# The first unit's maxima move from the front of the second attention into the first mixture

## The reference

```python
qkv = x @ Wqkv + bqkv
q, k, v = jnp.split(qkv, [D, D + KV], axis=-1)          # D = 256, KV = 64
q = q.reshape(b, s, H, HD)                              # H = 16 heads of HD = 16
k = jnp.tile(k.reshape(b, s, G, HD), (1, 1, H // G, 1)) # G = 4 shared keys
v = jnp.tile(v.reshape(b, s, G, HD), (1, 1, H // G, 1))
scores = jnp.einsum('bqhd,bkhd->bhqk', q, k) / HD
prob = jax.nn.softmax(scores, axis=-1)
out = jnp.einsum('bhqk,bkhd->bqhd', prob, v).reshape(b, s, D)
return out @ Wout + bout
```

## Time and profile before

| what | value |
| --- | --- |
| median of three runs | 2161.28 us (2160.81 to 2163.94) |
| profiled execution, its own time | 2152.04 us |
| span in the profile | 2150.0 us |
| mean granted clock, as a share of full speed | 0.986 |
| PE busy | 2080.3 us (97%) |
| DVE busy | 1460.8 us (68%) |
| ACT busy | 1221.3 us (57%) |
| POOL busy | 577.9 us (27%) |

### The profile page before, as it was taken

One profiled execution on the slowest core, in us unless ns is written; L12 is line 12 of the kernel. 1 busy time (PEld: TensorE's weight loads), 2 busy tenths in 40 slices (PEclk: granted clock), 3 DMA queues, 4 the chain that ended last, 5 costly groups with the idle time before them and its releaser, 6 DMA issues. The chain is left out here.

```text
span 2150.0 us, 33338 instructions
## 1 busy us (share of the span) xinstructions
PE 2080.3 (97%) x12160; PEld 1592.7 (74%) x12160; DVE 1460.8 (68%) x2761; ACT 1221.3 (57%) x2435; POOL 577.9 (27%) x679
## 2 busy tenths in 40 slices
PE   7999999999999999989999988999999899999997
PEld 6888888888788888877788873333334688778886
DVE  5666666677677666666656558999994556655555
ACT  5666666666556666554444443888887434444433
POOL 3444444444334444332222210000000112222221
PEclk9999999999999999999999996999999999999999
DMA  2000000000000000011111121101000111111111
GB/s 74 20 21 13 21 21 20 21 21 20 9 20 21 20 21 20 4 38 45 39 48 40 45 46 30 24 18 23 21 12 2 43 37 45 45 45 44 45 52 56
DMA packets 54309, 64.92 MB, mean 30 GB/s; under 512 B 9179, under 2 KB 34566, under 8 KB 54150
## 3 DMA queue, kind: packets, MB, share of 16 engines
q1 hardware_dynamic: 54150, 62.81, 10.4%
HBM read 52.68 MB, written 2.10 MB: 25 GB/s over the span
## 5 line engine op out<-in xcount | busy, mean ns | idle before, releaser
L862 POOL TENSOR_TENSOR a_pr<-a_pr,a_rinv 128x512 f32<-128x512 f32 (+3 forms) x384 | 312.8, 829 | 477.1 <-DVE a_rinv L1109 477.1
L86 PE MATMUL psum<-xh,g_hi_gu 128*128 128x512 f32 x928 | 377.8, 407 | 15.1 <-DVE xl L1092 8.9
L88 PE MATMUL psum<-xh,g_lo_gu 128*128 128x512 f32 x928 | 363.7, 392 | 0.0
L87 PE MATMUL psum<-xl,g_hi_gu 128*128 128x512 f32 x928 | 363.2, 391 | 0.0
L1830 DVE TENSOR_REDUCE a_negm<-psum 128x1 f32<-128x1024 f32 x256 | 309.7, 1223 | 17.5 <-PE psum L1697 16.5
L1190 POOL TENSOR_TENSOR g_lo_gu<-g_raw_gu,g_hi_gu 128x512 fp32r<-128x512 f32 x84 | 108.9, 1297 | 778.1 <-ACT g_hi_gu L1186 778.1
L1811 ACT ACTIVATE a_pt<-psum 128x512 f32<-128x512 f32 x512 | 276.4, 597 | 60.4 <-PE psum L1712 32.6
L1484 DVE TENSOR_TENSOR f_hl<-f_hid,f_hh 128x512 fp32r<-128x512 f32 x168 | 116.8, 695 | 238.4 <-ACT f_hh L1422 236.5
L1411 ACT ACTIVATE f_act_s<-psum,g_gu_bias 128x512 f32<-128x512 f32 x168 | 115.0, 685 | 277.7 <-PE psum L88 277.4
L1014 ACT ACTIVATE a_pr<-psum,a_negm 128x128 f32<-128x128 f32 (+7 forms) x256 | 190.2, 743 | 106.9 <-DVE a_negm L1099 102.9
L1021 ACT ACTIVATE a_pth<-psum 128x512 fp32r<-128x512 f32 (+3 forms) x384 | 174.9, 490 | 113.0 <-PE psum L921 110.3
(11 more groups left out here) (298 smaller groups left out, 4313.7 us busy)
## 6 DMA issues: line engine op xcount, KB each, us to landing
g_raw_gu<-in_gu SPq DMA_DIRECT2D x84, 256.0 KB, 2.8
f_raw_dn<-in_down SPq DMA_DIRECT2D x84, 128.0 KB, 2.0
g_raw_gu<-in_qkv SPq DMA_DIRECT2D x32, 256.0 KB, 2.8
a_wvr<-in_qkv SPq DMA_DIRECT2D x32, 128.0 KB, 2.4
a_wor<-in_o SPq DMA_DIRECT2D x32, 128.0 KB, 2.0
x_queries_qq<-x_qhi SPq DMA_DIRECT2D x128, 32.0 KB, 2.0
yT<-in_xT SPq DMA_DIRECT2D x4, 512.0 KB, 7.1
x_queries_qq<-x_qlo SPq DMA_DIRECT2D x64, 32.0 KB, 1.9
```

The source lines that it names most:

```text
L86: pe.matmul(out, a_hi, b_hi, start=first, stop=False)
L87: pe.matmul(out, a_hi, b_lo, start=False, stop=False)
L88: return pe.matmul(out, a_lo, b_hi, start=False, stop=last)
L862: pool.tensor_tensor(x, x, rinv[:, j:j + 1].to_broadcast([P, count * P]), ALU.mult).then_inc(p_done, 1)
```

## The change

Unit 0's 16 maxima leave `FIRST` and become side tasks of the first mixture, in tiles 37 to 44, two tasks for each half tile (one for each product, so both side banks). DVE reduces both banks in one instruction and raises `emptied` by two. For this the tasks before them are set closer: `root` at (31, 0) where it was at (31, 1), the `nb` tasks at (32, 0) to (33, 1), the `pj` and `vt` tasks from (34, 0) to (36, 1), and two `pj` tasks as second tasks at (33, 0) and (36, 0). SP copies the keys after `load(37)` and fetches unit 0's queries after `load(38)`; `p1` fetches units 1 and 2. In the second attention `turn(-1)` comes first, `FIRST` holds the eight maxima of unit 1, and PE adds two products to each of them whose result nothing reads. The copy of the second half's keys moves behind unit 0's maxima in SP's order. The query slots become four tensors, and `negm` is allocated outside the attention.

```diff
+class FirstMaxima:
+    COUNT = CH // P * G1
...
+    def tensor(self, pe, t, ring):
+        half, (q, g) = t[0], head_of(t[1])
+        p0, rows = g // 2 * HALFP, 3 * HD1
+        if t == (0, 0):
+            pe.wait_ge(self.side.k_in, self.side.K_LOADS)
+            pe.wait_ge(self.queries.q_in[0], 192)
+        o = free_bank(pe, ring, (self.name, t))
+        pe.matmul(o, self.queries.qq[0][p0:p0 + rows, g % 2, q * P:(q + 1) * P],
+                  self.side.ks[p0:p0 + rows, g % 2, half * CH:(half + 1) * CH], start=True, stop=True).then_inc(ring.filled, 1)
+    def scalar(self, act, t, ring):
+        pass
+    def vector(self, dve, t, ring):
+        if t[0] == 0:
+            return
+        q, g = head_of(t[1])
+        n = g * (CH // P) + q
+        dve.wait_ge(ring.filled, ring.count((self.name, t)))
+        dve.tensor_reduce(self.negm[:, 0, n:n + 1], self.both, AX.XY, ALU.max, negate=True).then_inc(ring.emptied, 2)
...
             for K in range(2, 2 * NT):
                 load(K)
+                for o in begins:
+                    if isinstance(o, QKVHalf) and K == NT + 9:
+                        o.sync(sp, ring)
+                    if isinstance(o, FirstMaxima) and K == NT + 10:
+                        o.queries.first(sp, o.side, ring)
             for o in begins:
                 if isinstance(o, QKVHalf):
-                    o.sync(sp, ring)
                     sp.wait_ge(o.k_in, o.K_LOADS)
...
-        FIRST = [(0, i) for i in range(STEPS)] + [(1, i) for i in range(STEPS // 2)]
+        FIRST = [(1, i) for i in range(STEPS // 2)]
...
-            sides[1].sync(sp)
-            queries.fetch(sp, Queries.AHEAD)
             for u in range(LAST + 1):
                 send_maxima(u)
                 if u == 0:
                     queries.fetch(sp, QSLOT - 1)
+                    sides[1].sync(sp)
...
+            turn(-1, False, True, room(ring.a_turn(-1, False, True)))
             for u, i in FIRST:
                 bank = room(ring.a_max())
                 for half in range(2):
                     maxima(u, i, half, bank)
-                if (u, i) == (0, STEPS - 1):
-                    turn(-1, False, True, room(ring.a_turn(-1, False, True)))
+                for n in range(2):
+                    pe.matmul(st_ps[:, n, :], ks[0][:, 0, 0:P], ks[0][:, 1, 0:CH], start=True, stop=True)
...
-                            **place(NT0 + 1, norm_slots(n1a) + PAUSE + tasks(x0, PROJECT))}
+                            **place(NT0 + 1, tasks(n1a, FORE + [("root",)]) + PAUSE + tasks(n1a, BACK) + tasks(x0, PROJECT[:6]))}
+                    for n, t in ((8, ("pj", 1, 0)), (14, ("pj", 1, 1))):
+                        plan[NT0 + 1 + n // 2, n % 2].append((x0, t))
+                    for n in range(m0.COUNT):
+                        plan[NT0 + 9 + n // 2, n % 2] = [(m0, (0, n)), (m0, (1, n))]
```

More of the change, by code:

```diff
@@ L1191, in remainder, with __init__, widen, fetch @@
                            ALU.subtract).then_inc(self.lo_done, 1)
+class Queries:
+    SLOTS, AHEAD = 4, 2
+    UNITS = [(b, j, c) for b in range(B) for j in range(H1 // G1) for c in range(S // CH)]
+    def __init__(self, ph, name, qhi, qlo):
+        self.ph, self.name, self.qhi, self.qlo = ph, name, qhi, qlo
+        self.qq = [ph.sb(f"{name}_qq0", [P, 2, CH], F32R)]
+        self.q_in = [ph.sem(f"{name}_q_in{s}") for s in range(self.SLOTS)]
+    def widen(self):
+        self.qq += [self.ph.sb(f"{self.name}_qq{s}", [P, 2, CH], F32R) for s in range(1, self.SLOTS)]
+    def fetch(self, sp, u):
+        b, j, c = self.UNITS[u]
+        t0, s = c * CH, u % self.SLOTS
+        for r in range(2):
+            for x, src in enumerate((self.qhi[b], self.qhi[b], self.qlo[b])):
+                for g in range(2):
+                    d0 = (j % 2 * G1 + r * 2 + g) * HD1
+                    p0 = r * HALFP + x * HD1
+                    sp.dma_start(self.qq[s][p0:p0 + HD1, g, :].bitcast(F32),
+                                 src[d0:d0 + HD1, j // 2, t0:t0 + CH].bitcast(F32)).then_inc(self.q_in[s], 16)
+    def sync(self, sp):
+        for u in range(1, 1 + self.AHEAD):
+            self.fetch(sp, u)
+    def first(self, sp, side, ring):
+        sp.wait_ge(ring.emptied, ring.count((side.name, ("pj", 0, 0))))
+        self.fetch(sp, 0)
@@ new lines, with head_of, __init__, has_bank @@
+GROUPS = (0, 2, 1, 3)
+def head_of(i):
+    return i // G1, GROUPS[i % G1]
+class FirstMaxima:
+    COUNT = CH // P * G1
+    def __init__(self, ph, name, queries):
+        self.name, self.queries = name, queries
+        self.negm = ph.sb(f"{name}_negm", [P, 2, self.COUNT])
+    @staticmethod
+    def has_bank(t):
+        return True
+    @staticmethod
+    def rounds(t):
+        return False
+    def tensor(self, pe, t, ring):
[16 more added lines that the diff above has]
+        dve.tensor_reduce(self.negm[:, 0, n:n + 1], self.both, AX.XY, ALU.max, negate=True).then_inc(ring.emptied, 2)
@@ L1269, in mixture @@
         after.ready = lambda s, ring: ((y_kept, (s // 2 + 1) * DT),)
+        for o in begins:
+            if isinstance(o, FirstMaxima):
+                o.both = side_ps[:, :, :]
         @block.sync
@@ L1510, in _, with grouped_attention @@
                             o.vector(dve)
[L1513 to L1541, removed]
+def grouped_attention(nc, tag, counters, queries, negm, sides, ks, vs, z, ident, psum, rear):
     ROWS = 3 * HD1
@@ L1614, in place @@
             def place(self):
-                if self.maxima < len(UNITS) * STEPS:
+                if self.maxima < MAXIMA:
                     self.n += 1
@@ L2007, in program @@
                 x.level(0)
[L2008 removed]
+                queries.widen()
                 with Phase(nc, "s1") as s:
```

33 lines of the change are left out of this document (16 added, 17 removed).

## The result

The changed kernel takes 2200.91 us (median of four, 2197.98 to 2205.19), the kernel before 2161.28 (2160.81 to 2163.94) on the same chip: ratio 1.0182, 95% interval 1.0164 to 1.0201. It is slower, as forecast, by 39.6 us where 10.7 were forecast, and outside the range (2160 to 2181). The profiled executions are 49.2 us apart in span (2150.0 and 2199.2).

A forecast was written before the change was run, and what follows sets the result against it. The prediction took PE to bound the mixture and DVE the maxima ahead of the second attention's loop. It summed 33.9 us paid in the mixture less 23.2 given back, +10.7, to 2172.0 us; range 2160 to 2181.

The forecast's parts named there:

- the waits: PE's new waits in the mixture: for side banks 16.8 us, for unit 0's queries 3.9, from closer tasks 5.8.
- 14.6 of 16.8: Tiles 38 to 44, (K, 0): PE waits 2.4 us each for side banks to be reduced, 16.8 us.
- 3.9 of 3.9: At (37, 0): the first maximum waits 3.9 us for unit 0's queries to land; bounds 1.5 and 5.9.
- 5.5 of 5.8: Tasks set closer: `root` +2.1 us, `pj` at (33, 0) 1.8, `pj` at (36, 0) 1.9; together 5.8.
- the products: Mixture: 32 added products of 512 columns at 0.23 us each, 7.4 us of PE.
- upper end of 12.5: Mixture: the added products at 0.39 us each, a whole length, if they don't overlap: 12.5 us.
- so my sum has no fall in it: Mixture: 2.4 us waits, shorter and between 9 us of unbroken products, add no slow-clock time to the sum.
- Rival 1: Clock falls at the waits: ten waits, each losing 1.7 us of products, make +17, 2189 us; chance 0.07.
- rival 2: Added products don't hold the clock, PE bounds ahead of the loop, only 16.8 us returned: +17.1, 2178; chance 0.07.
- I take 23.2, because PE has work there without a break: Second attention: the loop's tenth reduction ends 23.2 us earlier, with the added products free at full clock.
- The low end, 16.8: Second attention at 1.2 GHz: eight times 0.6 us lost and 1.5 us of loop start not saved; 16.8 returned.
- The 9.2 us: Median of the runs shown, 2161.28, is 9.2 us above the profiled execution; the same sum was put on it.

The follow-up runs named there:

- e2: Changed kernel, but DVE reduces the maximum of (K-1, 1) ahead of `keep_lo(K-1, 1)`, not behind `product(K, 0)`: 2175.89 us, ratio 1.0104.
- e8: Changed kernel with the reduction ahead of `keep_lo`, no unread products, and tasks from the root on half a tile later: 2157.82 us, ratio 1.0014.
- e13: Changed kernel with its unread products, reduction ahead of `keep_lo`, tasks half a tile later, ten unread products ending `p1`: 2144.73 us, ratio 0.9935.
- e7: Changed kernel with its unread products, reduction ahead of `keep_lo`, and ten unread products at the end of `p1`: 2167.67 us, ratio 1.0041.
- e5: Kernel before, with two unread products added to each of the 24 maxima ahead of the loop: 2184.23 us, ratio 1.0137.
- e10: Kernel before, with ten unread products back to back at the third step of the second attention's loop: 2154.56 us, ratio 0.9979.
- e1: Changed kernel without the two unread products at each of unit 1's eight maxima: 2193.98 us, ratio 1.0181.
- e11: Kernel of e8 with ten unread products back to back at the third step of the second attention's loop: 2149.22 us, ratio 0.9957.

## Why the prediction was wrong

**Right: the waits.** Each wait came where it was put and with its length (14.6 of 16.8, 3.9 of 3.9, 5.5 of 5.8), and `e2` and `e8` took them away by taking away what was named as their cause: DVE's order, and the closer tasks.

**Mis-sized: the products.** They were priced at 0.23 us, 7.4 in all. A pair costs 0.86 us with the steps into and out of it, and by the tiles of `e2` all 32 cost 14.5, above the upper end of 12.5. Why they follow more slowly than the mixture's own wasn't tried.

**Failed: "so my sum has no fall in it".** The forecast argued that waits of 2.4 us are shorter than every wait that a fall had followed and stand between unbroken products. Waits of 1.8 to 2.2 us were followed by a fall in tile after tile; with those behind the root and the queries they lost 17.1 us in all. Without them, with the same products, the clock was 1.00 in these tiles (`e2`). Rival 1 had this mechanism and priced it at 17 us, with a chance of 0.07. It came together with rival 2 (below); the forecast gave each a chance alone and had no case for both, 10.7 + 17 + 6.4 = 34.1 by its own prices. The Trainium skill, "TensorE: Matmul & The Clock Gate", section "HAM oscillation — how this bites in real kernels", says that waits between tiles can throttle the clock anew in each. In its example the wait is longer than a tile's work; this trace has it with waits of some 2.1 us in tiles of 13.85 us, with clocks of 0.66 to 0.68 in stretches of such tiles.

**Failed: "I take 23.2, because PE has work there without a break".** The 23.2 us themselves were right: `e13` gives back 23.0. But they hold at a full clock only, and with the wait of 2.5 us ahead of the block the clock falls in spite of the unread products (`e2`; with the wait filled it holds through the eight maxima, `e7`). At 1.2 GHz they make PE the bound (2.30 us a maximum) and don't bring the clock back (`e5`). The low end, 16.8, was too high as well: it charged the slow clock to the eight maxima, at 1.84 us each, and to 1.5 us of the loop's start, because in the profiled execution of before the loop had one slow step only the earlier trace rows. After, it had twelve, of 2.16 us in place of about 1.28. In the kernel before most of the slow time lies under 24 reductions that DVE paces; with 16 of them gone it lies in the loop, where PE paces.

**Not a cause of the miss: the base.** The 9.2 us between the profiled execution and the median were carried over as if they held for both kernels. They are the gap between before's two groups, which `e10` closes by acting on this loop alone. Without them the forecast would have been 2162.7, further from 2200.91.

Not settled: what decides whether a short wait is followed by a fall (1.8 us in the changed kernel and in `e1`), when the clock rises again in the loop (after 1 slow step in before's profile, 9 in `e1`, 12 in the changed kernel), why it fell at the loop's start in the profile of `e7` and not in that of `e13`, whose PE has gaps of 0.36 and 0.40 us there too, and whether the version of `e13` needs its unread products.

## What to carry to other kernels

Price a wait on an engine whose clock can fall at more than its length: here 14.6 us of waits in the mixture cost 25. Before moving work out of a stretch that another engine paces, ask what slow time that stretch was hiding; the next stretch may be paced by the slow engine. Products that are to hold a clock must begin before the gap that drops it: the same two products cost 7 us behind the gap, and with the gap filled they were part of the fastest version, though not shown to be needed there.

## What the runs showed of the hardware

PE was granted 1.2 GHz for 48 us (after) and for 80 us and more (`e5`) while it was busy almost without a break. In `e11` the clock rose within a burst of ten products of 128 rows and 512 columns, while `e8`, without it, stayed at 1.2 GHz until 1348. Waits of 1.8 to 2.2 us were followed by a fall 1.3 to 1.8 us after the restart, in each of seven tiles; another of 1.8 us in one profile and not in the next. One kernel's executions can form two groups 10 us apart with no change in its instructions; a profile shows only one of the groups.
